# A graph attention layer on one core: scaled rows in three bf16 parts, an fp32 spread with a one-hot made by ScalarE, and SyncE written out

## The reference

```python
h_trans = features @ Watt_w.T + Watt_b
h_src, h_dst = h_trans[src], h_trans[dst]
e_raw = jnp.sum(h_dst * jnp.tanh(h_src + e_r), axis=-1, keepdims=True)
e_ij = leaky_relu(e_raw * scaling)
exp_e = jnp.exp(e_ij - segment_max(e_ij, dst)[dst])
alpha = exp_e / (segment_sum(exp_e, dst)[dst] + 1e-09)
h_neigh = segment_sum(features[src] * alpha, dst)
h_out = leaky_relu((features + h_neigh) @ W1.T + b1 + (features * h_neigh) @ W2.T + b2)
out = layernorm(features + h_out)
```

## Time and profile before

| | us |
|---|---|
| time, median of 3 runs (3100.49 to 3104.06) | 3102.68 |
| time of the profiled execution | 3100.4 |
| its span | 3098.6 |
| PE busy | 1502.2 (48%) |
| DVE busy | 1290.4 (42%) |
| ACT busy | 1364.1 (44%) |
| POOL busy | 1570.8 (51%) |

### The profile page before, as it was taken

The page is one execution under the profiler, slowest core; times in us unless marked ns, Lnnn a source line. Parts: engine busy times, 40 slices in busy tenths (PEclk is TensorE's granted clock), DMA queues, the critical chain, the costliest instruction groups (busy, mean ns, idle before and its releaser), DMA issues.

```text
span 3098.6 us, 45175 instructions
## 1 busy us (share of the span) xinstructions
PE 1502.2 (48%) x11423; PEld 1295.1 (42%) x11423; DVE 1290.4 (42%) x7378; ACT 1364.1 (44%) x3900; POOL 1570.8 (51%) x1670
## 2 busy tenths in 40 slices
PE   4255444454444444544445444445444445444456
PEld 4244443444433444433444444444443344444345
DVE  2343444444444444434444444444434444344445
ACT  2244444444444444444444444444444444444446
POOL 4454455555555555455554555555555555555551
PEclk7555555555555555555555555555555555555555
DMA  4112222222222222222222222222222222222221
GB/s 169 51 52 59 58 59 56 60 59 60 58 59 61 55 59 59 58 59 61 55 59 58 59 58 61 55 59 59 59 58 61 61 54 59 59 58 61 61 60 30
DMA packets 169471, 187.26 MB, mean 60 GB/s; under 512 B 126146, under 2 KB 126358, under 8 KB 169315
## 3 DMA queue, kind: packets, MB, share of 16 engines
q0 software_dynamic: 53152, 107.98, 13.9%
q1 hardware_dynamic: 114897, 76.96, 9.0%
q10 hardware_dynamic: 1266, 0.93, 0.1%
HBM read 175.64 MB, written 10.07 MB: 60 GB/s over the span
## 4 chain that ended last, share of the span: by engine, by line
issue 50%; PE 47%; another core or an unknown queue 1%; DVE 1%; ACT 0%; DVEq 0%; POOL 0%; POOLq 0%
PE ps_acc L991 21%; PE ps_hd L945 13%; PE ps_hot L930 6%; PE ps_acc L1007 2%; PE ps_row L957 2%; PE ps_misc L972 1%; PE ps_acc L990 1%; PE ps_spare L998 1%; PE ps_misc L1002 1%; DVE hx L1151 0%; PE ps_row L898 0%; PE ps_row L894 0%; ACT hotT L730 0%; ACT weight L777 0%
## 5 line engine op out<-in xcount | busy, mean ns | idle before, releaser
L632 POOL DMA_INDIRECT got<-table,src_i x1631 | 1541.3, 945 | 1461.6 <-PE ps_acc L991 964.1
L945 PE MATMUL ps_hd<-h,hotT 128*128 128x64 bf16 x4983 | 410.3, 238 | 1371.6 <-issue 1370.5
L945 PEld LDWEIGHTS ps_hd<-h,hotT 128*128 128x128 bf16 x4983 | 328.7, 130 | 1457.4 <-issue 1456.1
L730 ACT ACTIVATE hotT<-ps_hot 128x1024 bf16<-128x1024 bf16 x222 | 211.9, 955 | 1387.5 <-PE ps_hot L930 1387.5
L991 PE MATMUL ps_acc<-got,weight 128*128 128x65 f32 x3322 | 706.8, 380 | 1.6 <-ACT weight L777 1.6
L991 PEld LDWEIGHTS ps_acc<-got,weight 128*128 128x128 f32 x3322 | 663.4, 294 | 54.0 <-issue 38.6
L777 ACT ACTIVATE weight<-hot,arg 128x128 f32<-128x128 bf16 x1661 | 507.3, 386 | 102.6 <-issue 64.3
L1244 DVE CUSTOM_DVE_ANT_0 edge<-edge,ps_hd 128x64 f32<-128x64 f32 x1661 | 265.0, 217 | 687.1 <-issue 430.1
L1233 DVE TENSOR_TENSOR edge<-edge,got 128x256 f32<-128x256 f32 (+1 forms) x444 | 179.4, 404 | 407.6 <-remote 278.6
L747 ACT ACTIVATE edge<-edge 128x256 f32<-128x256 f32 (+1 forms) x444 | 166.6, 394 | 133.3 <-issue 85.4
L930 PE MATMUL ps_hot<-ident,hot 128*128 128x128 bf16 x1661 | 198.0, 312 | 2.9 <-DVE hot L1222 2.9
(11 more groups left out here) (134 smaller groups left out, 1375.9 us busy)
## 6 DMA issues: line engine op xcount, KB each, us to landing
edge<-in_edge_attr SPq DMA_DIRECT2D x110, 480.0 KB
got<-table,src_i POOLq DMA_INDIRECT x1631
table<-hx SPq DMA_DIRECT2D x12, 512.0 KB
hw<-table SPq DMA_DIRECT2D x111, 32.0 KB
xw<-in_x SPq DMA_DIRECT2D x111, 32.0 KB, 1.9
out<-y_out SPq DMA_DIRECT2D x111, 32.0 KB
x_piece<-in_x SPq DMA_DIRECT2D x3, 768.0 KB, 4.3
row_i<-in_dst SPq DMA_DIRECT2D x110, 1.0 KB
```

The lines of the kernel that those rows point to most:

```text
L632: pool.indirect_dma_start(got[b.four][:, g, 0:2 * D], None, table, bass.IndirectOffsetOnAxis(ap=src_i[b.four][:, g:g + 1], axis=0))\
L730: act.activation(hotT[b.two][:, a:z, :], ps, ACT.Copy, bias=1.0, scale=-1.0).then_inc(hot_sb[p], 1)
L945: last = pe.matmul(expanded(g), hotT[b.two][:, g, :], h3[b.two][:, part, :], start=(part == 0), stop=(part == 2))
```

## The change

It has three parts.

**Scaled rows in parts.** ACT's 15 exponentials of 128 x 128 and the fp32 weights go. ACT makes `prob` (128 x 15); DVE multiplies the gathered features by it into `rest`, fp32 (`scale_rows`, 2 instructions of 520 and 455 elements per partition); ACT and DVE in turn split the result in three bf16 parts (`high_part`, `left_part`, `mid_part`, `low_part`, two each), and PE multiplies the one-hot `hot` by the three parts, 195 columns side by side, one bf16 matmul for each tile; a `tensor_reduce` of DVE adds the three. Since the gathered rows are not needed once they are scaled, POOL waits for `scaled` instead of `summed`.

**An fp32 spread.** `hotT` is no longer a transpose of `hot`: SP loads the window's 1920 ids into all partitions (`dst_all`, 983 KB written), ACT makes |id - node| in bf16 (`offsets`) and 1 minus that, cut at zero, in fp32 (`mark_nodes`). PE's spread is one fp32 matmul for each tile with `hw` itself; the 15 transposes, the copies out of PSUM and `split_h` go. `ps_hd` has four banks, one a chunk.

**SP written out.** All 111 steps of SP stand one behind the other, with addresses fixed at build time except the node bases, which are loaded once for each window. The two `row_i` loads go.

```diff
         edge_max = sb("edge_max", [P, TILES])
         arg = sb("arg", [P, TILES])
-        weight = sb("weight", [P, TILES, P])
...
+        parts = sb("parts", [P, TILES, 3, D + 1], BF16)
...
-        ps_hd = [bank(f"ps_hd{k}") for k in range(NP)]
-        ps_hot = [bank(f"ps_hot{k}", BF16) for k in range(NP)]
+        ps_hd = [bank(f"ps_hd{k}") for k in range(CHUNK)]
...
-                        sp.wait_ge(consts, 5)
                         sp.wait_ge(scored[NC - 1], nxt.n - 1)
                     load_edges(nxt)
...
-                if exists(nxt):
-                    if follows(nxt, 2):
-                        sp.wait_ge(consts, 5)
-                        sp.wait_ge(ids_set, nxt.n - 1)
-                    load_row(nxt)
...
+                    load_nodes(b, bases_at[b.n])
...
+                    sp.wait_ge(ids_set, ahead.n - 1)
+                    sp.wait_ge(off_set[NP - 1], ahead.n - 1)
+                    load_dst_all(ahead)
+                    sp.wait_ge(hd_ready[NC - 1], ahead.n - 1)
+                    load_h(ahead, bases_at[ahead.n])
                 if exists(third):
-                    store_nodes(third, stores_at)
+                    store_nodes(third, bases_at.pop(third.n))
...
+                for n in range(-1, WINDOWS):
+                    step(*(at_block(0, n + j) for j in (-3, -2, -1, 0, 1, 2, 3)))
...
-                        pool.wait_ge(summed[c // 2], freed)
+                        pool.wait_ge(scaled[c // 2], freed)
...
+            def offsets(b, p):
...
+                t = tiles(b)
+                if p == 0:
+                    act.wait_ge(dst_all_in[b.two], (b.twos + 1) * 16)
+                    act.wait_ge(node_set, b.n + 1)
+                if follows(b, 1):
+                    act.wait_ge(hotT_built[p], b.n)
+                ids = dst_all[b.two][:, 1:1 + t * P].rearrange("p (e g) -> p g e", g=t)
+                act.activation(off[p][:, 0:z - a, :], ids[:, a:z, :], ACT.Abs, bias=node[b.two][:, 0:1])\
+                    .then_inc(off_set[p], 1)
...
+            def mark_nodes(b, p):
...
+                act.wait_ge(off_set[p], b.n + 1)
                 if follows(b, 2):
...
+                    act.wait_ge(consts, 5)
+                    act.wait_ge(hd_ready[PIECE_CHUNKS[p][-1]], b.n - 1)
+                act.activation(hotT[b.two][:, a:z, :], off[p][:, 0:z - a, :], ACT.Relu, bias=ones[:, 0:1], scale=-1.0)\
+                    .then_inc(hotT_built[p], 1)
...
+                act.wait_ge(arg_done, b.n + 1)
+                act.activation(prob[:, 0:tiles(b)], arg[:, 0:tiles(b)], ACT.Exp).then_inc(prob_set, 1)
...
+            def high_part(b, p):
+                a, z = piece(b, p)
+                act.wait_ge(scaled[p], b.n + 1)
+                if follows(b, 1):
...
                     act.activation(carry_weight[:, :], carry_arg[:, :], ACT.Exp)
-                for g in range(*cols(b, c)):
-                    last = act.activation(weight[:, g, :], hot[b.four][:, g, :], ACT.Exp,
-                                          bias=arg[:, g:g + 1], scale=-MASKED)
-                last.then_inc(weights_done[c], 1)
+                act.activation(parts[:, a:z, 0, :], rest[:, a:z, :], ACT.Copy).then_inc(rest_high[p], 1)
+            def mid_part(b, p):
+                a, z = piece(b, p)
+                act.wait_ge(rest_left[p], b.n + 1)
+                act.activation(parts[:, a:z, 1, :], rest[:, a:z, :], ACT.Copy).then_inc(rest_mid[p], 1)
...
+                    probabilities(prev)
                 if exists(nxt):
-                    split_h(nxt, 0)
-                    copy_hot(nxt, 0)
+                    offsets(nxt, 0)
+                    mark_nodes(nxt, 0)
...
-                    weigh(prev, 2)
-                    weigh(prev, 3)
+                    high_part(prev, 0)
+                    high_part(prev, 1)
                 if exists(b):
                     tanh(b, 1)
+                if exists(prev):
+                    mid_part(prev, 0)
                 if exists(nxt):
-                    split_h(nxt, 1)
-                    copy_hot(nxt, 1)
...
+                    offsets(nxt, 1)
+                    mark_nodes(nxt, 1)
+                    take_last(nxt)
+                if exists(prev):
+                    mid_part(prev, 1)
...
+            def expand(b, c):
+                pe.wait_ge(hotT_built[c // 2], b.n + 1)
+                if c == 0:
+                    pe.wait_ge(h_in[b.two], (b.twos + 1) * 16)
                 if follows(b, 1):
-                    pe.wait_ge(hot_sb[p], b.n)
-                for g in range(*piece(b, p)):
-                    k = g - piece(b, p)[0]
-                    last = pe.transpose(ps_hot[p][:, k * P:(k + 1) * P],
...
+                    pe.wait_ge(scored[c], b.n)
+                for g in range(*cols(b, c)):
+                    last = pe.matmul(expanded(g, c), hotT[b.two][:, g, :], hw[b.two][:, :], start=True, stop=True)
+                last.then_inc(hd_ready[c], 1)
...
+            def sum_edges(b, p):
...
+                pe.wait_ge(rest_low[p], b.n + 1)
+                for g in range(*piece(b, p)):
...
+                    last = pe.matmul(a_parts, hot[b.four][:, g, :], parts[:, g, :, :].rearrange("p a d -> p (a d)"),
                                      start=(g == 0), stop=(g == tiles(b) - 1))
-                if c % 2 == 1:
-                    last.then_inc(summed[c // 2], 1)
+                last.then_inc(summed[p], 1)
...
-                    expand(b, 0)
-                    expand(b, 1)
-                if exists(nxt):
-                    transpose_hot(nxt, 0)
-                    transpose_hot(nxt, 1)
-                if exists(prev):
-                    sum_edges(prev, 0)
-                    sum_edges(prev, 1)
+                    for c in range(NC):
+                        expand(b, c)
                 if exists(before):
                     transpose_sum_prod(before)
                 if exists(prev) and carried(prev):
                     take_carry(before)
                 if exists(prev):
-                    sum_edges(prev, 2)
+                    sum_edges(prev, 0)
+                    sum_edges(prev, 1)
                 if exists(b):
                     lay_rows(b)
-                if exists(prev):
-                    sum_edges(prev, 3)
-                if exists(b):
...
                     dve.wait_ge(hot_built[NC - 1], b.n)
+                if follows(b, 2):
+                    dve.wait_ge(consts, 5)
+                    dve.wait_ge(off_set[NP - 1], b.n - 1)
+                column = node_all[:, b.n:b.n + 1] if b.known else node_all[:, bass.ds(b.n, 1)]
+                dve.tensor_copy(node[b.two][:, :], column).then_inc(node_set, 1)
                 column = base_all[:, b.n:b.n + 1] if b.known else base_all[:, bass.ds(b.n, 1)]
                 chain("base", dve.tensor_copy(base[:, :], column), b)
...
+                    dve.wait_ge(summed[NP - 1], b.n - (BUFS - 1))
...
-                    ALU.not_equal).then_inc(hot_built[c], 1)
+                    ALU.is_equal).then_inc(hot_built[c], 1)
...
+            def scale_rows(b, p):
+                a, z = piece(b, p)
+                dve.wait_ge(prob_set, b.n + 1)
+                dve.tensor_tensor(rest[:, a:z, :], got[b.four][:, a:z, D:2 * D + 1],
+                                  prob[:, a:z].rearrange("p (g d) -> p g d", d=1).to_broadcast([P, z - a, D + 1]),
+                                  ALU.mult).then_inc(scaled[p], 1)
+            def left_part(b, p):
+                a, z = piece(b, p)
+                dve.wait_ge(rest_high[p], b.n + 1)
+                dve.tensor_tensor(rest[:, a:z, :], rest[:, a:z, :], parts[:, a:z, 0, :], ALU.subtract)\
+                    .then_inc(rest_left[p], 1)
+            def low_part(b, p):
+                a, z = piece(b, p)
+                dve.wait_ge(rest_mid[p], b.n + 1)
+                dve.tensor_tensor(parts[:, a:z, 2, :], rest[:, a:z, :], parts[:, a:z, 1, :], ALU.subtract)\
+                    .then_inc(rest_low[p], 1)
...
+                    chain("sum", dve.tensor_reduce(sums[:, :], a_parts.rearrange("p (a d) -> p d a", a=3), AX.X, ALU.add), b)
...
+                if exists(prev):
+                    scale_rows(prev, 0)
+                    scale_rows(prev, 1)
...
-                if exists(nxt):
-                    split_h(nxt, 0)
                 if exists(b):
                     set_gaps(b)
+                    dot(b, 0)
                     add(b, 1)
-                    dot(b, 0)
+                if exists(prev):
+                    left_part(prev, 0)
+                    left_part(prev, 1)
+                if exists(b):
+                    dot(b, 1)
                     add(b, 2)
-                    dot(b, 1)
-                if exists(nxt):
-                    split_h(nxt, 1)
+                if exists(prev):
+                    low_part(prev, 0)
+                if exists(prev):
+                    low_part(prev, 1)
```

221 lines of the change are left out of this document (91 added, 130 removed).

## The result

| | time, us | ratio to before |
|---|---|---|
| before, 4 runs (3100.49 to 3104.06) | 3102.29 | |
| after, 4 runs (2810.71 to 2818.54) | 2814.99 | 0.9073 (0.9058 to 0.9089) |

The change makes the kernel 287 us faster. I had forecast 3156 us and a range down to 2930.

What follows compares the result with a forecast made beforehand. Bound: the gather burst with its slow issue, and the chain starting the next. First burst 131, 106 periods of 27.7 (2936), last stretch 16, end 71: span 3154, with 1.8 outside 3156 us; range 2930 to 3360.

Steps and rivals of the forecast that it cites:

- The step that failed: During a gather burst, every engine's issue crawls from about 5 us after its start until 3.8 us after its last gather starts.
- the stretch: Part of each POOL gather burst in which instructions issue slowly; said to end 21.2 us after the burst's start.
- Rival C: PE's row matmuls finish inside the stretch, scan and y_out move into it: period 26.0 us, 2976 us; chance 0.28.
- A: The forecast itself: scan follows the end of the stretch, period 27.4 to 28.4 us, 3124 to 3230 us; chance 0.40.
- B: The crawl catches DVE's dots, so dot 2 and 3 run after the stretch: period 29.4, 3336 us; chance 0.23.
- D: Nothing moves, DVE's longer way being as long as PE's was: 3097 to 3109 us; chance 0.05.
- What releases a burst: POOL's next burst waits for DVE's first scale_rows instead of PE's sums, 4.7 us after y_out.
- Costs of each engine: Added work per window: DVE pairs 1.2 us each, PE's spread 6.4; a window without gathers takes 17.6 us.
- SP: Unrolled SP and the extra 983 KB load a window cost 0; up to 2 us if on the path.
- Rival E: DVE's scaling and splitting hold up POOL's gathers for 3.6 us: period 31.3, 3540 us; chance 0.04.

Runs made afterwards that it cites:

- last_spread: Changed kernel with PE's spread moved out of the step's start, chunk by chunk into the step ahead, on a chip with the stretch: 3041.96 us, ratio 0.9772.
- a_gate: Changed kernel with the old gate, POOL waiting for PE's sums (summed) instead of DVE's scaling: 2969.46 us.
- a_act24: Changed kernel with 24 more one-element activations in each step of ACT, behind high_part: 2824.21 us.
- b_sp: Kernel before with only SP written out in place of its loop: 3101.46 us, against 3105.29 for the kernel before.
- again_one_part: Kernel before with one of the three spread matmuls (15 in place of 45), on a chip without the stretch: 2113.45 us, ratio 0.9997.
- again_after: The changed kernel itself, unedited, beside the kernel before on a chip without the stretch: 2205.17 us, ratio 1.0440.

## Why the prediction was wrong

**The step that failed** is "from about 5 us after its start until 3.8 us after its last gather starts, issue of every engine crawls". I took both ends as fixed to the burst, because in the one kernel that I had every burst looks the same. Only the end is: +21.2, 21.4, and 21.6 in the windows shown of before, after and last_spread. The beginning moves with the program: +5 before, right behind `y_out` (1534.24, SP's store at 1535.49, the burst from 1529.85), close behind `y_out` in a_gate (SP's transfers start 2 us apart from 1420.95 on), which comes 4.6 us into the burst, about +15 in most windows of after, by +12.4 in last_spread. Nor does every engine crawl: in after PE runs its spread through the stretch. A trace in which each window repeats the last can't tell a fixed delay from a fixed place in the step; I should have given the second a chance of its own. All that I put behind +5 by this step fell with it: `lay_rows` ended at +12.4, not +21.2.

**Rival C** had the right direction and the right test (`lay_rows` ends before +20.8), but kept the early beginning of the stretch, so its 2976 us are 161 too many. Its mechanism, rows laid inside the stretch because the engines share what crawls, is not what happened: rows, scan and `y_out` came ahead of the stretch, and a_act24 speaks against the sharing. Its 0.28 was too low. A, B and D fell: no dot stands in or behind the stretch.

**What releases a burst.** Right as to who (DVE's scaling), wrong in size: 1438.15 - 1428.00 = 10.2 us from `y_out`, forecast 4.7. I thought that no slow stretch lay on this way; now 4.69 us of it lie ahead of `dst_rel`, and 0.46 and 0.31 in the two small gaps on either side. With these 5.46 taken off, 4.7 is left. The measured period is 14.0 + 10.2 = 24.2, forecast 23.0 + 4.7 = 27.7.

**Costs of each engine.** Scaling and `left_part` took 1.23 and 1.24 us a pair (1.2), `low_part` 0.70 + 0.64 (1.2), the spread 6.61 (6.4). The offsets took 1913 ns: the bound of "twice" was the truth. The last two windows took 19.2 and 16.4 us (17.6), and the end behind the last burst 82.3 (87). The first burst came at 139 us (131). These terms held, to within 10 us of 2815.

**SP.** Cost 0 and gain 0: right (b_sp, 3101.46 against 3105.29).

**Rival E** was dismissed too easily. Its size of 3.6 us a window was wrong, its mechanism is there: the mean gather went from 945 to 997 ns, 0.8 us a window. I judged it by the `add` of the earlier trace rows, and in the order of before an `add` seldom lengthens a gather (14 of 391 in again_one_part); the new instructions run longer and do so in 327 of 582 cases. With the stretch these 0.8 us hardly count, since POOL waits anyway; without it they are the whole result, +4.4%.

**What stays open.** What starts the stretch. SP's store, its register load and its loop don't, nor do 24 more activations bring it on, nor does PE's row of spreads. Nor is it the loading of code, as far as the trace records it: in before the instruction queue has packets in 82 of the 106 periods, and the other 24 are as long (27.26 us on average against 27.35). ACT loads tables twice a step, and the kernel without table loads ran on a chip without the stretch, so that was not tested. The second load can't be the start in last_spread, for in each of its 102 late windows the scan was already due before that load began (in the window shown 1426.6 against 1426.98). The first load (1424.26 there), the loops of the other engines and SP's other transfers stay possible. Nor do I know why some chips lack it: of seven comparisons on chips, before took 3099 to 3105 us in four and 2109 to 2114 in three, nothing between.

## What to carry to other kernels

When one interval in a trace repeats, list what its beginning could be tied to (the transfer, a place in the program, a count of instructions) and price the change by each, because a change that moves the one against the other tells them apart with some hundred us. Releasing a buffer earlier can be worth more than its own wait where it moves a burst of indirect gathers against work that stands still beside them (about 155 us here, on chips with the stretch). Where gathers of POOL are the bound, count for each DVE instruction how many of the gathers beside it get longer; taking one of two operands away cured `low_part`, but not `left_part`. And measure on more than one chip before you say that a kernel got faster.

## What the runs showed of the hardware

- The kernel before took 3099 to 3105 us on some chips and 2109 to 2114 on others, the changed one 2815 and 2205, the latter at the same mean granted clock of TensorE, 0.508 in both. The trace of the changed kernel has the slow stretch in one case, and not in the other, where POOL never waits. Of before there is no trace of its own from the second kind of chip; again_one_part stands for it.
- In the stretch of before, PE's single matmuls start 2.80, 1.40 and 1.42 us apart (the rows below, and 1551.09 in the earlier trace rows), about four and two times 0.70 us; `edge` on SP's queue took 0.71 and 0.72 us above. In after PE runs 30 passes in it without a gap. The stretch ends 21.2 to 21.6 us after the first of 15 gathers starts, 3 to 4 us after the start of the last.

```profile
1545.47 0.21 PE L945 MATMUL ps_hd<-h,hotT 128*128 128x64 bf16 x1 [2.59 <-issue]
1548.27 0.21 PE L945 MATMUL ps_hd<-h,hotT 128*128 128x64 bf16 x1 [2.58 <-issue]
1549.67 0.21 PE L945 MATMUL ps_hd<-h,hotT 128*128 128x64 bf16 x1 [1.20 <-issue]
```

- A gather of 128 rows of 512 bytes took 0.94 us alone and, in the rows above, 1.14 to 1.33 beside a DVE instruction with two operands in SBUF; in again_after 328 of 724 such overlaps cost time. Beside `left_part` with one operand it took 1.10 to 1.12.
- ACT took 1.91 us for 128 x 1024 int32 values that lie 60 bytes apart, and 0.96 for the copy of 128 x 1024 bf16.
